# A pairwise-attention kernel: the PSUM layout, the pair layout and the load of the gather table changed together

## The chip, the cores and the metric

The kernel runs on one core of a Trainium2 chip. The metric is device microseconds of one execution, median of several; smaller is better. TensorE (PE) multiplies, VectorE (DVE) and ScalarE (ACT) compute elementwise, GpSimd (POOL) issues indirect gathers, SyncE (SP) issues plain DMAs. Every engine runs its own instruction list in order and meets the others through counting semaphores.

## The reference, cut to what matters

`VOCAB` is 12500, there are 32 fields, a batch of 2048, and embeddings of 64 numbers.

```python
V = emb_v[x]                                  # x: (32, 2048) indices, V: (32, 2048, 64)
iu, ju = np.triu_indices(32, k=1)             # the 496 pairs of fields
VV = V[iu] * V[ju]
hid = relu(einsum('pbk,kh->pbh', VV, at_w) + at_b)      # 64 -> 64
score = einsum('pbh,ho->pbo', hid, at_h)
pooled = sum(VV * score, axis=0)
logit = pooled @ p + w0 + sum(w1[x], axis=0)
prob = sigmoid(logit)
```

Every index outside 0..12499 is wrapped or clamped as the array library does. All arithmetic is float32.

## The kernel before

Because `pooled @ p` is linear, the kernel never forms `VV * score`. It computes the scores of all pairs, and apart from them the Gram products `sum_k p[k] V[i,k] V[j,k]`, multiplies the two and sums over the pairs.

The batch is worked in 32 *fills* of 64 samples (`FILLS`). A fill holds two groups `g` of 16 samples, and each group twice, on the lower and on the upper 64 partitions (`half`). In a fill there are 16 *rounds*: eight steps `s` times two groups, in the order of `ORDER`. Fill 0 and fill 31 are written out, fills 1 to 30 are a loop over two fills.

A round goes through three engines:

- DVE writes the products of one step: `X` (L348, two instructions, one for each of the two pieces that `segments(s)` gives). Step `s` pairs the fields 2s and 2s+1 with all later ones, and the mirror step fills the rest, so a round always has 2 x 512 columns. DVE may be eight rounds ahead (`X_SLOTS`).
- PE multiplies them with `w_sb`: `hidden` (L476), four matmuls of 64 x 64 weights and 512 columns into one of two PSUM slots of `Z` (`Z_SLOTS` 2). Every float32 matmul shows as two passes in the trace, so as two MATMUL rows and two LDWEIGHTS rows.
- ACT adds the bias and applies the relu from `Z` to `H` (L424), 1024 columns. `hidden` of round r waits for the relu of round r-2.

Beside the rounds, PE has in each fill, in program order:

- `scores` (L497): the column `hcol`, placed in a 32-wide weight, times `H`, into the PSUM bank `S`. There are four column tiles of the array (two groups, two halves), each with 128 x 32 weights, and each step needs one matmul a piece and tile: 496 and 16 columns for step 0, 464 and 48 for step 1, and so on to 272 and 240. They stand after rounds 7, 9, 15, and after round 1 of the next fill, two steps at a time.
- `clear_scores` (L485) ahead of the first scores: four bf16 matmuls with zeros open the sums in `S`.
- `grams` (L515): for each of 16 samples and two groups a matmul of 128 x 64 weights (`pV`) and 32 columns (`V`) into the bank `G`, eight of them after each of the rounds 3, 5, 11 and 13.
- `turn` (L455): eight 128 x 128 transposes of the gathered rows of the next fill into the two banks of `TR`, after round 8.

ACT copies `TR` to `V` (L369) after the relu of round 8 and writes `pV` from `TR` (L376) after that of round 15. DVE masks the Gram products (L317), multiplies them with the scores (L323) and sums (L326) in rounds 4, 5 and 6 of the next fill. `S`, `G`, `TR` and the two slots of `Z` are all eight PSUM banks.

POOL gathers the rows of a fill, 16 indirect DMAs of 128 rows (L233), two fills ahead. Fills 0 and 1 gather from `emb_v` itself. The later ones gather from two tables in DRAM, whose rows have the `w1` entry before or behind the embedding (260 bytes): at the start SP loads all of `emb_v` in one DMA of 3104 KB (L191), DVE and ACT join it with `w1` in SBUF (L333, L384), and SP stores both tables (L202), 6.3 MB in all. `w1` of fills 0 and 1 is gathered at the end (L242). The last steps are `linear_term` (L556), the sums of `part` (L566) and a sigmoid (L439).

## Time and profile before

| | |
|---|---|
| median of 3 runs | 920.51 us (919.03 to 921.53) |
| profiled execution | 918.6 us, of which the span of the engines is 916.8 us |
| PE busy | 866.9 us, 95% of the span |
| DVE, ACT, POOL busy | 708.2, 675.2, 563.4 us |
| chain of work that ended last | PE 92%, POOL 4%, DMA 2% |

The profile's page gives busy times, forty slices of the span, the chain that ended last, the costliest groups of instructions and the DMAs. The trace can be asked for any stretch: the chain in order of time, the instructions of one engine merged where they follow each other, the waits, the DMA queues. A busy PE means only that a matmul was in flight: a row's time holds the latency of the pipeline as well, so the pace is read from starts, or from the pieces of the chain.

### The profile page before, as it was taken

How to read it: one execution, taken by the hardware profiler on the slowest of the kernel's cores; microseconds unless marked ns; L12 is line 12 of the kernel's file. 1: busy time of each engine (PE TensorE's matmuls, PEld its weight loads, DVE VectorE, ACT ScalarE, POOL GpSimd, SP SyncE). 2: the span in 40 equal slices, each digit the busy share in tenths (PEclk: the TensorE clock that was granted, in tenths of full speed). 3: DMA queues.
4: the chain of work that ended last, by engine and by line, in shares of the span. 5: the costliest groups of instructions: out<-in, count | busy, mean ns of one | idle time of the engine just before them, and what ended most of it. 6: DMA issues, size and time to landing. Idle time of an engine off the chain costs nothing.

```text
span 916.8 us, 27050 instructions
## 1 busy us (share of the span) xinstructions
PE 866.9 (95%) x10676; PEld 339.1 (37%) x10676; DVE 708.2 (77%) x1179; ACT 675.2 (74%) x771; POOL 563.4 (61%) x584
## 2 busy tenths in 40 slices
PE   0549999999999999999999999999999999999998
PEld 0113333333433333333333333333333333333333
DVE  3555789777778977777898777779877777987772
ACT  3327777787877778787777788777778877777884
POOL 5717767555566765565676556556665555666770
PEclk9878999999999999999999999999999999999999
DMA  8972222222222222222222222222222222222000
GB/s 169 174 143 25 25 26 21 19 19 19 18 21 22 22 19 19 19 19 20 22 23 19 19 19 19 20 21 22 21 19 19 19 19 20 23 19 20 8 1 2
DMA packets 19638, 27.35 MB, mean 30 GB/s; under 512 B 10646, under 2 KB 10662, under 8 KB 18982
## 3 DMA queue, kind: packets, MB, share of 16 engines
q0 software_dynamic: 17408, 17.07, 25.0%
q1 hardware_dynamic: 1566, 10.02, 2.8%
q8 instruction: 11, 0.18, 0.1%
q10 hardware_dynamic: 648, 0.03, 0.0%
q14 instruction: 5, 0.04, 0.0%
HBM read 20.59 MB, written 6.51 MB: 30 GB/s over the span
## 4 chain that ended last, share of the span: by engine, by line
PE 92%; POOL 4%; DMA 2%; issue 1%; DVE 0%; SPq 0%; ACT 0%; POOLq 0%; DVEq 0%
PE Z L476 53%; PE S L497 26%; PE G L515 8%; PE TR L455 4%; POOL rows L233 3%; DMA rows<-in_L_rec_emb_v_dram,idx_stage 2%; PE S L485 1%; PE TR L556 0%; DMA idx_raw<-in_r_x_dram 0%; SPq L188 0%; ACT y_sb L439 0%; DVE prod L323 0%; DVE part L326 0%; POOL idx_stage L221 0%; PE TR L566 0%
## 5 line engine op out<-in xcount | busy, mean ns | idle before, releaser
L424 ACT ACTIVATE H<-Z,bias 128x1024 f32<-128x1024 f32 x512 | 546.5, 1112 | 192.2 <-PE Z L476 191.2
L348 DVE TENSOR_TENSOR X<-V 128x992 f32<-128x992 f32 (+15 forms) x1024 | 640.2, 696 | 24.2 <-ACT V L369 20.8
L233 POOL DMA_INDIRECT rows<-table,idx_stage x480 | 489.2, 1019 | 167.4 <-issue 144.5
L476 PE MATMUL Z<-X,w_sb 64*64 64x512 f32 x4096 | 517.2, 608 | 1.5 <-DVE X L348 1.2
L497 PE MATMUL S<-H,score_w 128*32 128x496 f32 (+15 forms) x4096 | 248.3, 383 | 0.0
L476 PEld LDWEIGHTS Z<-X,w_sb 64*64 64x64 f32 x4096 | 123.7, 131 | 182.4 <-issue 174.8
L497 PEld LDWEIGHTS S<-H,score_w 128*32 128x32 f32 x4096 | 111.2, 110 | 184.4 <-issue 139.8
L323 DVE TENSOR_TENSOR prod<-S,gram 128x512 f32<-128x512 f32 x32 | 22.1, 692 | 159.0 <-PE S L497 159.0
L515 PEld LDWEIGHTS G<-V,pV 128*64 128x64 f32 x2048 | 70.0, 137 | 103.8 <-issue 103.8
L221 POOL COPY idx_stage<-idx 128x16 uint32 (+1 forms) x32 | 7.1, 222 | 143.5 <-ACT w_all L392 122.6
L376 ACT ACTIVATE pV<-TR,pcol 64x512 f32<-64x512 f32 x128 | 87.0, 680 | 2.5
L515 PE MATMUL G<-V,pV 128*64 128x32 f32 x2048 | 84.3, 225 | 0.0
L455 PE MATMUL TR<-ident,rows 128*128 128x128 f32 x256 | 36.9, 289 | 44.6 <-DMA rows<-in_L_rec_emb_v_dram,idx_stage 44.6
L455 PEld LDWEIGHTS TR<-ident,rows 128*128 128x128 f32 x256 | 28.7, 146 | 70.6 <-issue 63.0
L369 ACT COPY V<-TR 128x512 f32<-128x512 f32 x64 | 34.2, 587 | 24.5 <-PE TR L455 24.5
L242 POOL DMA_INDIRECT w_all<-in_L_rec_w_dram,idx x32 | 33.5, 1048 | 9.8 <-issue 9.8
L233 POOL DMA_INDIRECT rows<-in_L_rec_emb_v_dram,idx_stage x32 | 32.7, 1023 | 10.8 <-issue 9.2
L317 DVE TENSOR_TENSOR gram<-G,upper 128x512 f32<-128x512 f32 x32 | 21.8, 681 | 8.1 <-PE G L515 8.1
L326 DVE TENSOR_REDUCE part<-prod 128x512 f32 (+1 forms) x32 | 21.8, 680 | 0.0
L485 PEld LDWEIGHTS S<-zeros 128*32 128x32 bf16 x128 | 3.3, 92 | 26.0 <-issue 26.0
L485 PE MATMUL S<-zeros 128*32 128x512 bf16 x128 | 12.8, 390 | 0.0
L392 ACT COPY w_all<-rows 128x8 f32 x60 | 9.3, 202 | 0.7
(38 smaller groups left out, 42.6 us busy)
## 6 DMA issues: line engine op xcount, KB each, us to landing
rows<-table,idx_stage POOLq DMA_INDIRECT x480
table<-joined SPq DMA_DIRECT2D x2, 1592.5 KB
table<-joined SPq DMA_DIRECT2D x2, 1560.0 KB
raw<-in_L_rec_emb_v_dram SPq DMA_DIRECT2D x1, 3104.0 KB, 11.7
rows<-in_L_rec_emb_v_dram,idx_stage POOLq DMA_INDIRECT x32, 12.3
w_all<-in_L_rec_w_dram,idx POOLq DMA_INDIRECT x32
idx_raw<-in_r_x_dram SPq DMA_DIRECT2D x4, 64.0 KB, 2.2
raw_w<-in_L_rec_w_dram SPq DMA_DIRECT2D x1, 48.5 KB, 13.4
```

What stands on the lines that cost most here:

```text
L233: pool.indirect_dma_start(out=rows[parity][:, g * FILL_M + m, half, c0:c1], out_offset=None, in_=source[half] if joint else source, in_off ...
L242: pool.indirect_dma_start(out=w1_all[:, Q, n:n + 1], out_offset=None, in_=w1, in_offset=at).then_inc(w1_first, 16)
L323: nc.vector.tensor_tensor(prod[:, :, :], S[:, :, :], gram[:, :, :], ALU.mult).then_inc(prod_ready, 1)
L348: last_one = nc.vector.tensor_tensor(xo, vj, vi.unsqueeze(3).to_broadcast(shape), ALU.mult)
L369: nc.scalar.copy(V[parity][:, g, :, :], TR[:, g, :].rearrange("p (b f) -> p b f", f=FIELDS)).then_inc(v_ready, 1)
L376: nc.scalar.activation(pV[parity][k, g, :, half, :, :], TR[k, g, :].rearrange("p (b i c) -> p b c i", c=2, i=FIELDS // 2), ACT.Copy, scale ...
L424: nc.scalar.activation(H[:, r % H_SLOTS, :, :], Z[:, r % Z_SLOTS, :, :], ACT.Relu, bias=bias[:, 0:1]).then_inc(hid_ready, 1)
L455: last = nc.tensor.transpose(TR[:, g, 128 * m:128 * m + 128], embs[:, g * FILL_M + m, 1:1 + 2 * EMB], ident[:, :])
L476: last = nc.tensor.matmul(Z[64 * par:64 * par + 64, r % Z_SLOTS, half, :], w_sb[k, :], X[k, r % X_SLOTS, par, :], start=True, stop=True)
L485: nc.tensor.matmul(S[32 * Q:32 * Q + 32, :, :], zeros[:, 0:32], zeros[:, :].rearrange("p (b j) -> p b j", j=FIELDS), start=True, stop=False)
L497: last = nc.tensor.matmul(S[at:at + 32, :, j0:FIELDS], score_w[:, slot, :], hid.rearrange("p (b j) -> p b j", j=nj), start=False, stop=(s ...
L515: last = nc.tensor.matmul(G[64 * g:64 * g + 64, b, :], pV[parity][:, g, b, :, :, :].rearrange("p h c i -> p (h c i)"), V[parity][:, g, b, ...
```

## The change

- PSUM: `TR`, `S` and `G` go. `Z` gets three slots (`Z_SLOTS` 3, six banks) as a ring over rounds (`z_slot`), in which `turn` takes one place before round 8. Two banks `SG` alternate by fill and hold first the Gram products and then, once DVE has taken those, the scores.
- Waits: `hidden` of round r waits for the relu of round r-3 instead of r-2 (`z_before`), except round 0, 1, 8 and 9 (r-2), and round 10, which waits for the copy to `V`.
- Pairs: `segments` now splits each row of 32 columns in two parts, so that a group's `X` of a step is 16 x 32 in place, and the scores of a step and tile are one matmul of 512 columns. The first one starts the sum (`start=(s == 0)`), so `clear_scores` goes. The order of the rounds is both groups of one step after each other, except in the first half of fill 0 (`FIRST_ORDER`).
- Scores stand after rounds 3 (steps 6 and 7 of the fill before), 7, 11 and 15, with a semaphore step each. All Gram products of the next fill stand in one piece after round 15.
- `grams` has four column tiles in place of two: 64 matmuls of 128 x 32 weights and 32 columns a fill, where there were 32 of 128 x 64 weights. `pV` is one buffer, written by ACT from `V` in two instructions of 1024 columns, before rounds 10 and 14, with a weight column that is zero for the other half (`pmask`). `V` is copied in one instruction.
- DVE: masking takes three instructions (`mask_gram`) instead of one, since the new pair layout wraps around; multiply and sum stand before rounds 10 and 12.
- Table: one table with rows of 66 numbers (`w1`, embedding, `w1`), gathered by an index times 66 plus 0 or 1. SP loads `emb_v` straight into the joined layout, in 12 DMAs of 128 x 8 pieces of 256 bytes, once the rows of fill 0 have arrived, and stores 3.3 MB. POOL writes the two `w1` columns. Fills 0 to 2 gather from `emb_v`.
- POOL: the loop is written out, without the copy of the indices; from fill 4 on each group of four gathers waits for `z_ready` of a round (`PACE`), and one `w1` gather follows each fill.
- `linear_term` uses four row tiles of 32 and stands behind the last scores.

The diff, cut to this:

```diff
-X_SLOTS, Z_SLOTS, H_SLOTS = 8, 2, 8
+X_SLOTS, H_SLOTS, Z_SLOTS = 4, 4, 3
...
 def segments(s):
-    n = FIELDS - 1 - 2 * s
-    return [(s, FIELDS - n, n, 0), (STEPS * 2 - 1 - s, n, FIELDS - n, GROUP * n)]
+    low = 2 * s + 1
+    return [(2 * s, low, FIELDS, 0), (HALF_FIELDS + 2 * s, 0, low, HALF_FIELDS)]
...
+def z_slot(r):
+    return (r if r < TURN_BEFORE else r + 1) % Z_SLOTS
+TURN_SLOT = TURN_BEFORE % Z_SLOTS
+def z_before(r):
+    if r == 2:
+        return -3
+    if r < 2:
+        return r - 2
+    return r - 2 if TURN_BEFORE <= r < TURN_BEFORE + 2 else r - 3
...
+            for g in range(2):
+                sp.wait_ge(first_rows[g], 16 * GATHERS // 2)
+            sp.dma_start(tail[:, :, 1:1 + EMB], last_rows[0]).then_inc(tail_loaded, 16)
+            for k, (c0, c1) in enumerate(HALF_CHUNKS):
+                for c in range(c0, c1):
+                    sp.dma_start(joined[:, c, :, 1:1 + EMB], chunks(emb_v, c, c + 1)[:, 0, :, :]).then_inc(joined_loaded[k], 16)
...
+            gather(2)
+            pool.wait_ge(rows_turned, 1)
+            pool.wait_ge(idx_ready, 4)
+            pool.wait_ge(table_stored, 16 * 3)
+            gather(3)
+            for t in range(4, FILLS):
+                pool.wait_ge(rows_turned, t - 2)
                 pool.wait_ge(w1_kept, 2 * (t - 3))
-                gather(t, parity, table)
+                gather(t, paced=True)
+                gather_w1(1)
...
+                if not first:
+                    dve.wait_ge(v_ready, t)
+                for r, (s, g) in enumerate(FIRST_ORDER if first else ORDER):
...
+                    if r == 8:
+                        mask_gram(t, parity)
+                    if r == 10 and not first:
+                        weigh(t - 1, 1 - parity)
+                    if r == 12 and not first:
+                        sum_pairs(t - 1)
...
+                    xs = X[:, s % X_SLOTS, :, g * COLS:(g + 1) * COLS].rearrange("p c (b j) -> p c b j", j=FIELDS)
...
+                        xo = xs[:, :, :, p0:p1]
...
-            def clear_scores(t, first):
...
             def products(t, parity, first, last):
                 for r in range(ROUNDS):
-                    hidden(t, r, first)
+                    if r == TURN_BEFORE and not first and not last:
+                        pe.wait_ge(hid_ready, ROUNDS * t + TURN_BEFORE - Z_SLOTS + 1)
+                        turn(t + 1, 1 - parity)
+                    hidden(t, r, first, last)
                     if first and r == 3:
-                        turn(0, 0, (1,))
-                        keep_busy(8)
-                    if r == 8 and not last:
-                        pe.wait_ge(pv_ready, 4 * t + 4)
-                        turn(t + 1, 1 - parity)
+                        first_turn(1)
+                    if first and r == 5:
+                        grams(0, 0)
+                    if first and r == ROUNDS - 1:
+                        pe.wait_ge(hid_ready, ROUNDS - 2)
+                        turn(1, 1)
...
+                    if r == ROUNDS - 1 and not last:
+                        grams(t + 1, 1 - parity)
...
+            def grams(t, parity):
+                pe.wait_ge(pv_ready, 2 * t + 2)
+                if not (isinstance(t, int) and t <= 1):
+                    pe.wait_ge(prod_ready, t - 1)
+                for b in range(GROUP):
                     for g in range(2):
                         for half in range(2):
                             at = 32 * (2 * g + half)
+                            last = nc.tensor.matmul(SG[parity][at:at + 32, b, :],
+                                                    pV[:, g * GROUP + b, half, :, :].rearrange("p c i -> p (c i)"),
+                                                    V[parity][:, g * GROUP + b, :], start=(b == 0), stop=(b == GROUP - 1),
+                                                    skip_group_check=True)
+                last.then_inc(gram_ready, 1)
```

PE in the steady loop, from the Gram products behind round 5 (before) through the scores behind round 7. `Z` is `hidden`, `G` the Gram products, `S` the scores:

```order
L515 MATMUL G<-V,pV 64x32 x8
L469 REGISTER_ALU
L476 MATMUL Z<-X,w_sb 64x512 x4
L469 REGISTER_ALU
L476 MATMUL Z<-X,w_sb 64x512 x4
L485 MATMUL S<-zeros 32x512 x4
L497 MATMUL S<-H,score_w 32x16x31 x4
L497 MATMUL S<-H,score_w 32x16 x4
L497 MATMUL S<-H,score_w 32x16x29 x4
L497 MATMUL S<-H,score_w 32x16x3 x4
```

Now, the last two rounds of a fill (14 and 15) with what stands behind them and the first round of the next:

```order
L544 MATMUL Z<-X,w_sb 64x512 x4
L533 REGISTER_ALU
L544 MATMUL Z<-X,w_sb 64x512 x4
L558 MATMUL SG<-H,score_w 32x512 x8
L565 ISA
L572 MATMUL SG<-V,pV 32x32 x64
L533 ISA
L538 REGISTER_ALU
L544 MATMUL Z<-X,w_sb 64x512 x4
```

What moved: the 8 Gram matmuls that stood between pairs of rounds are gone from there, and 64 narrower ones stand once, directly behind scores of the same tile shape; two steps of scores are 8 matmuls where they were 16 and 4 with zeros.

DVE in the steady loop before, rounds 4 to 6, with the masking, the multiply and the sum of the fill before (its waits stand beside the rows):

```order
L317 TENSOR_TENSOR gram<-G,upper 128x512 [waits gram_ready]
L342 REGISTER_ALU
L348 TENSOR_TENSOR X<-V 128x2x464 [waits z_ready]
L348 TENSOR_TENSOR X<-V 128x2x48
L322 REGISTER_ALU [waits gram_masked]
L323 TENSOR_TENSOR prod<-S,gram 128x512 [waits scored]
```

DVE now, from the last product of round 7 to the multiply before round 10:

```order
L410 TENSOR_TENSOR X<-V 128x2x16x7
L364 REGISTER_ALU
L365 TENSOR_TENSOR gram_last<-SG,lower_last 128x256 [waits gram_ready]
L367 TENSOR_TENSOR gram<-SG,upper_first 128x512
L371 TENSOR_TENSOR gram<-gram,gram_last 128x16x16 [waits gram_halves]
L400 REGISTER_ALU
L410 TENSOR_TENSOR X<-V 128x2x16x23 [waits z_ready]
L410 TENSOR_TENSOR X<-V 128x2x16x9
```

What moved: the masking is of the current fill and stands before round 8, in three instructions; the multiply of the fill before stands two rounds later.

## Rows read from the trace of the kernel before

**Rows 1.** The page's busy times, and the granted clock of PE in 40 slices.

```profile
PE 866.9 (95%) x10676; PEld 339.1 (37%) x10676; DVE 708.2 (77%) x1179; ACT 675.2 (74%) x771; POOL 563.4 (61%) x584
...
PEclk9878999999999999999999999999999999999999
```

**Rows 2.** The chain in order of time, one fill: start us, us, engine, tile, line.

```profile
412.88 0.33 PE S L485 x4
413.21 1.76 PE S L497 x32
414.97 1.02 PE Z L476 x8
415.99 1.02 PE TR L455 x8
...
418.03 1.86 PE S L497 x32
419.89 1.88 PE Z L476 x16
421.77 0.59 PE G L515 x16
...
432.44 2.07 PE Z L476 x16
...
439.49 0.33 PE S L485 x4
```

**Rows 3.** Weight loads in time, scores of step 0: start us, us, count.

```profile
413.45 0.12 PEld L497 LDWEIGHTS S<-H,score_w 128*32 128x32 f32 x4 [0.30 <-issue]
413.87 0.18 PEld L497 LDWEIGHTS S<-H,score_w 128*32 128x32 f32 x12 [0.30 <-issue]
```

**Rows 4.** DVE in order of time in one fill.

```profile
410.70 15.06 DVE L348 TENSOR_TENSOR X<-V 128x672 f32<-128x672 f32 x24
425.67 0.68 DVE L317 TENSOR_TENSOR gram<-G,upper 128x512 f32<-128x512 f32 x1
...
432.50 0.69 DVE L323 TENSOR_TENSOR prod<-S,gram 128x512 f32<-128x512 f32 x1 [4.95 <-PE S L497]
...
434.31 0.68 DVE L326 TENSOR_REDUCE part<-prod 128x512 f32 x1
```

**Rows 5.** ACT in order of time in the same fill.

```profile
417.14 1.06 ACT L369 COPY V<-TR 128x512 f32<-128x512 f32 x2
...
428.05 2.79 ACT L376 ACTIVATE pV<-TR,pcol 64x512 f32<-64x512 f32 x4
...
431.20 2.12 ACT L424 ACTIVATE H<-Z,bias 128x1024 f32<-128x1024 f32 x2
```

**Rows 6.** The chain at the start.

```profile
15.54 0.94 POOL rows L233
...
16.79 0.94 POOL rows L233
...
48.47 18.83 DMA rows<-in_L_rec_emb_v_dram,idx_stage
...
82.92 1.88 PE Z L476 x16
```

**Rows 7.** DMA queues from 29 to 66 us: packets, MB, share of 16 engines.

```profile
q0 software_dynamic: 608, 0.62, 51.4%
q1 hardware_dynamic: 562, 6.28, 39.9%
```

**Rows 8.** The same, one steady fill, 412.8 to 439.4 us.

```profile
q0 software_dynamic: 479, 0.50, 23.6%
```

**Rows 9.** All engines in order of time at the end.

```profile
898.70 3.66 PE L556 MATMUL TR<-w_all,pick 128*4 128x128 f32 x32
...
912.08 0.69 DVE L323 TENSOR_TENSOR prod<-S,gram 128x512 f32<-128x512 f32 x1 [4.92 <-PE S L497]
912.81 0.69 DVE L326 TENSOR_REDUCE part<-prod 128x16 f32<-128x512 f32 x1
```

488 lines of the change are left out of this document (247 added, 241 removed).

## The prediction

> **What bounds the kernel now.** I read the page first, then one steady fill. PE is busy 95% of the span and its granted clock is at the upper level (2.4 GHz) from the fifth slice on [rows 1], so after some 90 us the time is PE's own list of work. The chain in order of time shows of what that list is made: one fill lasts from 412.88 to 439.49, 26.61 us, every piece of it on PE [rows 2]. The pieces are worth more than the busy sums, for they hold what it costs to change between kinds of matmul. Two rounds of `hidden` in one block take 1.88, a round alone 1.02 [rows 2]: so a round is 0.86, and a block costs 0.16 more than its rounds. The turn fits (1.02), and so do the scores: 1.86 for two steps whose columns are those of two rounds. So the columns count and not the matmuls: the scores of a step are 16 passes, a round is 8, and both cost the same. Twice in a fill a block of rounds is longer than 1.88 by more than 0.1 (2.07 in the rows, 2.01 the other), a wait for a relu with only two slots.
>
> The other engines have room. DVE writes 12 rounds in 14.97 us (410.70 to 425.67), 1.25 each, and idles 4.95 us [rows 4]. ACT needs 1.06 for a relu in a row, 1.06 for `V`, 2.79 for `pV` [rows 5].
>
> **The change in a steady fill, part by part.**
>
> Zeros: the piece of 0.33 holds an edge; without it the scores behind it cost 1.86 in place of 1.76. Gone: 0.23.
>
> Gram products: four blocks of 0.59, 2.36 in all, go. With them the blocks of `hidden` that they parted join: nine blocks before (after rounds 1, 3, 5, 7, 8, 9, 11, 13, 15), four now, so 5 x 0.16 = 0.80 goes too. The 64 new matmuls stand behind scores of the same tile shape, so I give them no edge. They are 32 passes over four tiles, each with a load of 32 columns and 32 moving columns. The trace has no such pass; what is nearest? Scores of step 0 have 16 moving columns, the same tiles and loads. There, 12 loads (three passes of four tiles) start within 0.18, of which the last load itself is 0.11 to 0.12 [rows 3], so from pass to pass there is 0.03. Below that I see no reason for a gain. Above, the old Gram passes, two tiles with loads of 64 columns, take (0.59 - 0.16)/8 = 0.055. If the load sets the pace (64 columns 0.055, 32 columns 0.03), the new pass is 0.03. I take it: 32 x 0.03 = 0.96, bounds 0.9 and 1.76.
>
> Scores as one matmul: the passes of step 0 with 16 columns cost 0.03 where their columns are worth 0.014, the others nothing. Gone: 0.05. This part of the change, taken alone, brings next to nothing.
>
> Third slot: the longer blocks (0.19, 0.13 and three times 0.05) become 1.88-like. Gone: 0.35. Is nothing later? Write a fill from its start by these pieces: rounds 0 to 3 until 3.59, scores 5.45, rounds 4 to 7 9.04, scores 10.90, turn 11.92, rounds 8 to 11 15.51, scores 17.37, rounds 12 to 15 20.96, scores 22.82, Gram products 23.78. ACT from the turn on: `V` until 13.0, relus 8 and 9 15.1, `pV` (1024 columns, 1.06 like a relu, at most 1.40, half of 2.79) 16.3, relus 10 and 11 18.4, `w1` 18.7, relu 12 19.8, relu 13 20.8, `pV` 22.0. Round 15 begins at 20.1 and needs relu 12: 0.3 to spare. The Gram products begin at 22.8 and need `pV`: 0.8 to spare. Both hold, the first barely: each 0.1 that ACT is later there costs 3 us in 31 fills.
>
> DVE: 16 x 1.25 = 20.0, mask, multiply and sum 0.68 + 0.69 + 0.68 [rows 4], and two new instructions of 256 columns, between 0.34 and 0.68 each: 22.7 to 23.4. Below 23.8, so DVE stays hidden, with 2% to 5% left where it had 19%. Its new waits: the mask waits for Gram products that end with the fill, when eight rounds are still ready; the multiply waits until 5.45 for the scores, and DVE then stands still 1 to 1.5 us with rounds 2 to 9 written ahead. PE needs round 10 at 13.6, DVE has it at about 7.5.
>
> POOL: 17 gathers at 1.25 (16.79 - 15.54 in [rows 6]) are 21.3 of 23.8; rows are due a third of a fill after the last is paced. Hidden.
>
> Sum: 26.61 - 0.23 - 2.36 - 0.80 - 0.05 - 0.35 + 0.96 = **23.78 us a fill**, 2.83 less.
>
> **The start.** Fill 1 begins at 82.92 now [rows 6], held up by the rows of fill 1: the gathers are issued by 48.47 and land 18.83 us later [rows 6], while the two tables (6.28 MB) are stored [rows 7]. Changed: no 3.1 MB load stands before the first gathers, and the table load starts when those have landed. The eighth gather starts at 15.54, so group 0 is there at some 18.5 and not at 24.8, group 1 at 29. The gathers of fill 1 end at 48.5 and those of fill 2 at 69. The table meanwhile: 12,288 pieces of 256 bytes. Bounds for a piece: a gathered row costs 0.236 x 16 x 26.6 / 2048 = 0.049 us of an engine [rows 8], and stored bytes in large packets 0.399 x 592 us / 6.28 MB = 0.010 us per 256 bytes [rows 7]. Over 16 engines that is 8 to 38 us; with gathers beside it, and then 3.3 MB of stores (8 to 16), the table is ready between 50 and 110 us, and I take 65. Then it is later than nothing: POOL has its turn for fill 3 at 69, rows by 91, and PE wants them at 95.
>
> The rows of fill 1 land between 50.5 and 60 in this lighter traffic; turn, `V`, two `pV` and Gram products follow one another there (some 6 us), so fill 1 begins at 56 to 66, I take 60. Fill 2 begins at 84.5, against 109.5 before: 25 us gained, bounds +5 and 30.
>
> **The end.** `linear_term` stood in PE's path with 3.66 us [rows 9]. It now runs with four row tiles while DVE multiplies and sums (0.69 + 0.69). Fill 31 has no turn and no Gram products for a next fill. From the start of fill 31 (82.92 + 30 x 26.61 = 881.2) to the end of the span were 35.6; now four blocks of rounds and of scores 21.8, last scores 1.8, tail 5.1: 28.7. Gained: 7.
>
> **Total**, against the profiled execution (span 916.8, time 918.6): 25 + 29 x 2.83 + 7 = 114, so 804.6. The median is 1.9 above that execution; I say **806**.
>
> **Rivals.**
>
> 1. *A floor per matmul.* The old Gram blocks have 16 passes in 0.43 us if each is counted singly, 0.027 each. If that is a pace of instructions and not of loads, 128 are 3.5 and not 0.96: 26.3 a fill, 806 + 79 = 885. For it: the profile shows no long run of such small matmuls that go faster. Against it: the 12 loads of [rows 3] with their matmuls, but these may be drawn from a filled queue. Chance 0.08. The Trainium skill, page TensorE: Matmul & The Clock Gate, Part 1, "Wait — 56ns, not 53.3ns?", says that starts never come closer than about 25 ns however small the matmul; by it the block would be 3.2 us and the time some 875. The rows with 16 columns speak against applying it to four tiles at once.
> 2. *The pass keeps the pace of the two-tile one*, 0.055: 1.76 for the block, 806 + 31 x 0.8 = 831. Chance 0.10.
> 3. *DVE becomes the bound.* `X` is now written in short runs of 1 to 31 numbers, where a run was whole before. From 1.30 to 1.33 a round on DVE sets the pace; at 1.38 (a tenth more) a fill is 24.7 and the time 834. For it: the new layout. Against it: what it reads was already in such short runs, at 1.25. Chance 0.08.
> 4. *The table is late.* At 100 us instead of 65, gathers end at 122 and turn 3 waits 27 us: 833. Chance 0.06.
> 5. *New waits of ACT and PE* at the tight places above, 0.3 to 0.7 a fill: 815 to 828. Chance 0.05.
> 6. *Slower than before*: the same runs on DVE, but worse. The point from which it decides: 26.6 + 1.0 (start and end gained, a fill's share) - 2.7 (its other work) = 24.9 for 16 rounds, 1.56 a round, a quarter above the rows. At 1.65 the time is about 970. Chance 0.04, of which 0.01 for a time at the point itself.
>
> **How the numbers follow.** The forecast has 0.59, and is itself 796 to 818. The range leaves out the floor per matmul, the slower case and a little of the forecast's own low end, and reaches over cases 2 to 5: 795 to 850. Faster by over 0.3% (what a measurement of this kernel can tell from no change) are all cases but the last: 0.96, within 0.3% 0.01, slower 0.03.
>
> **What will show it.** In the chain of the changed kernel the 16 rounds of a fill should be four pieces of some 3.6 us, two steps of scores with Gram products 2.8; 3.6 and more for Gram products alone is case 1, 1.8 case 2. Steady fills should follow one another by 23.8. If PE idles for `X`, DVE's cadence tells between case 3 and the forecast; if for `H`, it is case 5. PE waiting for rows behind 70 us is case 4. I am wrong in kind if PE shows gaps in the steady fills that none of these names.

## The result, and the profile after

The changed kernel took 868.44 us (864.78 to 874.28, four runs) against 920.78 us (919.03 to 921.53) for the kernel before in the same comparison: 0.944 of the time, 95% interval 0.9385 to 0.9495. It is faster, as forecast, but 62 us above the forecast of 806 and 18 us above the range. The profiled execution took 867.35 us, its span 865.6. The sets of runs in which the experiments were made differ: in some the kernel before took 1383 to 1427 us, not 920, and each experiment is read beside the kernel before of its own set. Where executions of one kernel lay over 1.5% above its fastest, the ratios with an interval leave these out as far as enough others remain; the medians and ranges hold all.

The page after, where [rows 1] stand for before: busy time and share of the span, and PE's granted clock in 40 slices.

```profile
PE 800.9 (93%) x10552; PEld 292.6 (34%) x10552; DVE 722.4 (83%) x1242; ACT 642.8 (74%) x672; POOL 604.9 (70%) x574
...
PEclk9889959999999999999999999999999999999999
```

PE lost 66 us of work and is still the bound. DVE has 14 us more. The sixth slice (108 to 130 us) has the clock down to half.

The chain in order of time, two fills of after, against [rows 2]: start us, us, engine, tile, line. L544 is `hidden`, L558 `scores`, L508 the turn, L572 the Gram products.

```profile
388.65 1.20 PE SG L572 x72
389.85 0.08 issue
389.93 0.38 PE SG L572 x11
390.32 0.42 issue
390.73 3.66 PE Z L544 x32
394.40 1.85 PE SG L558 x16
...
401.70 1.02 PE Z L508 x8
...
413.62 1.12 PE SG L572 x79
414.74 0.06 issue
414.80 3.66 PE Z L544 x32
```

The long blocks, the scores and the turn are what the sum had. The Gram products are not: the block at 388.65 takes 1.66 and is followed by 0.42 in which PE waits for nothing that the profile shows ("issue"); the next block takes 1.12 with 0.06. The starts of single passes show the pauses inside the longer block as gaps of 0.2 to 0.3 us, behind the 50th pass here (the 46th to the 59th in the steady fills) and again some 60 later. I read them as waits of PE for its own instructions: no row names that, but the experiments below bear it out. In 26 steady fills the block took 1.65 us in the middle, and one fill followed another by 24.80 us on the mean where 23.78 was forecast.

DVE in order of time, one piece of the same stretch (against [rows 4]); the bracket is idle time and what ended it.

```profile
420.38 0.69 DVE L378 TENSOR_TENSOR prod<-SG,gram 128x512 f32<-128x512 f32 x1 [1.63 <-PE SG L558]
```

DVE waits here for PE's scores, and not PE for DVE. It sets nothing.

The chain at the start, against [rows 6].

```profile
31.57 5.69 SPq L234
...
58.91 12.07 SPq L234
...
85.71 4.54 DMA joined<-in_L_rec_emb_v_dram
...
90.27 10.10 DMA table<-joined
...
101.16 0.94 POOL rows L268
...
120.94 4.71 DMA rows<-table,joint_idx
...
125.78 1.94 PE Z L508 x8
```

SP needs from 31.57 to 85.7 us to issue the twelve loads of the joined table (5.69 us for the first, 12.07 for the seventh), the last lands at 90.25, the stores at 100.37. Only then does POOL gather the rows of fill 3, which PE awaits for 17.9 us. Its turn takes 1.94 in place of 1.02, at the lower clock level (1.2 GHz, granted clock 0.50), and the four rounds behind it 5.13 in place of 3.66 (0.70 on the mean): PE had stood still just before. Up to here the changed kernel has gained nothing: turn 3 starts at 125.78, in the kernel before at 123.2.

One block has a pause while POOL stands still. The rows of PE for the Gram products behind fill 1:

```profile
95.06 0.64 PE L572 MATMUL SG<-V,pV 128*32 128x32 f32 x48
95.91 0.89 PE L572 MATMUL SG<-V,pV 128*32 128x32 f32 x80 [0.22 <-issue]
```

POOL issued nothing between 66.95 and 101.16, but the stores of the table kept the transfer engines full (1.04 of their time). The longest wait of PE for nothing that the profile shows, 2.99 us from 68.59, also falls into that stretch, with the engines at 0.97 (the last gathers' packets and the loads).

**Where the 62.8 us went** (span 865.6 against the 802.8 that the prediction implies):

| term | forecast | measured | us more |
|---|---|---|---|
| fill 2 begins | 84.5 | 96.9 (its turn's start, less the wait and 10.9) | 12.4 |
| wait of turn 3 for the table's rows | 0 | 17.9 | 17.9 |
| fill 2's start to fill 31's, without that wait | 29 x 23.78 | 29 x 24.88 | 31.9 |
| fill 31 and the tail | 28.7 | 29.2 | 0.5 |

### The profile page after: what moved, and what is told of

The parts are those of the page before. It is cut to its first block, busy times and chain, and to the rows that moved or that the text cites. A ratio compares the mean times of both kernels' runs of the same rounds, so it can differ in the third digit from the quotient of the medians.

```text
span 865.6 us, 26461 instructions
## 1 busy us (share of the span) xinstructions
PE 800.9 (93%) x10552; PEld 292.6 (34%) x10552; DVE 722.4 (83%) x1242; ACT 642.8 (74%) x672; POOL 604.9 (70%) x574
## 4 chain that ended last, share of the span: by engine, by line
PE 84%; SPq 6%; POOL 3%; DMA 3%; issue 2%; ACT 0%; DVE 0%; POOLq 0%
PE Z L544 49%; PE SG L558 25%; SPq L234 6%; PE SG L572 5%; PE Z L508 4%; POOL rows L268 3%; DMA table<-joined 1%; DMA rows<-in_L_rec_emb_v_dram,idx 1%; DMA rows<-table,joint_idx 1%; DMA joined<-in_L_rec_emb_v_dram 1%; DMA idx_raw<-in_r_x_dram 0%; PE Z L627 0%; SPq L220 0%; PE Z L615 0%; SPq L231 0%
## 5 line engine op out<-in xcount | busy, mean ns | idle before, releaser
L268 POOL DMA_INDIRECT rows<-table,joint_idx x464 | 510.4, 1100 | 197.5 <-issue 120.4
L544 PE MATMUL Z<-X,w_sb 64*64 64x512 f32 x4096 | 476.2, 601 | 11.8 <-issue 9.0
L544 PEld LDWEIGHTS Z<-X,w_sb 64*64 64x64 f32 x4096 | 156.8, 133 | 280.2 <-issue 274.7
L558 PE MATMUL SG<-H,score_w 128*32 128x512 f32 x2048 | 247.5, 600 | 0.1
L558 PEld LDWEIGHTS SG<-H,score_w 128*32 128x32 f32 x2048 | 53.8, 109 | 182.0 <-issue 103.8
L436 ACT ACTIVATE pV<-V,pmask 128x1024 f32<-128x1024 f32 x64 | 80.7, 1264 | 0.1
L572 PEld LDWEIGHTS SG<-V,pV 128*32 128x32 f32 x4096 | 50.0, 110 | 31.1 <-issue 26.1
L572 PE MATMUL SG<-V,pV 128*32 128x32 f32 x4096 | 56.6, 200 | 4.0 <-ACT pV L436 1.0
L268 POOL DMA_INDIRECT rows<-in_L_rec_emb_v_dram,idx x48 | 46.3, 964 | 18.0 <-issue 14.2
L508 PE MATMUL Z<-ident,rows 128*128 128x128 f32 x248 | 35.6, 289 | 24.3 <-DMA rows<-table,joint_idx 17.9
L279 POOL DMA_INDIRECT w_all<-in_L_rec_w_dram,idx x48 | 46.4, 966 | 14.6 <-issue 14.6
L508 PEld LDWEIGHTS Z<-ident,rows 128*128 128x128 f32 x248 | 28.0, 146 | 50.3 <-issue 38.6
```

The source lines that it names most:

```text
L268: pool.indirect_dma_start(out=rows[t % 2][:, g * FILL_M + m, half, c0:c1], out_offset=None, in_=source, in_offset=bass.IndirectOffsetOnAxi ...
L279: pool.indirect_dma_start(out=w1_all[:, Q, n:n + 1], out_offset=None, in_=w1, in_offset=at).then_inc(w1_first, 16)
L436: nc.scalar.activation(pV[:, :, half, :, :], V[parity][:, :, :].rearrange("p b (i c) -> p b c i", c=2), ACT.Copy, scale=pmask[:, half:half ...
L508: last = nc.tensor.transpose(Z[:, TURN_SLOT, g, 128 * m:128 * m + 128], embs[:, g * FILL_M + m, 1:1 + 2 * EMB], ident[:, :])
L544: done = nc.tensor.matmul(Z[64 * par:64 * par + 64, z_slot(r), half, :], w_sb[k, :], X[k, s % X_SLOTS, par, COLS * g:COLS * g + COLS], sta ...
L558: last = nc.tensor.matmul(SG[parity][at:at + 32, :, :], score_w[:, s, :], hid.rearrange("p (b j) -> p b j", j=FIELDS), start=(s == 0), sto ...
```

## Experiments

Runs of one set follow each other on one chip and share the kernel before. It took 1383 to 1427 us in the sets of e1 to e16, e19 and e20 (**1400 sets** below) and 916 to 922 us in the comparison above and in the set of e17 and e18 (**920 sets**). The changed kernel stands in the 1400 sets as e5 and e16. The 1400 sets ran on four chips, the set of e17 and e18 on a fifth; whether the chip makes the difference, no run tells. Many expectations give times for the 920 case and met a 1400 set, so there only their direction and the blocks can be held against them.

**e5_after_again and e16_after_third: the changed kernel in 1400 sets.** No edit.

> The changed kernel as it is, once more, so that the kernels beside it stand against it under the same conditions. The kernel before took 1422 us beside the first four experiments and 920 us beside the two kernels' own comparison. If the four columns of a gram block or a round are starved by the supply of TensorE's instructions, this kernel shows it again: gram block of 128 passes 1.65 us where before takes about 920 us, and then 865 to 874 us in all; gram blocks of 4 to 7 us and a steady fill above 30 us where before takes about 1420 us. If the long times beside the first four came from those kernels' own edits, this one gives 868 us beside any time of before.

> The changed kernel as it is, beside the three above. 868 us where before takes 920, 1130 to 1180 us where it takes about 1400.

Measured: 1172.99 us (1168.49 to 1175.51) beside 1423.62, ratio 0.824 [0.821, 0.827]; 1173.61 beside 1418.70, 0.827 [0.826, 0.829]. The steady fill is 34.1 us, the Gram block 6.9. In e5's chain a normal block of that set:

```profile
541.00 0.45 PE SG L572 x39
541.45 0.39 issue
541.84 0.28 PE SG L572 x4
...
545.87 1.17 issue
547.04 0.93 PE SG L572 x39
547.97 6.00 PE Z L544 x32
```

The chain has 39 passes up to the first wait (by the starts of single passes the first gap stands behind the 48th); then PE gets about five at a time, each 0.75 us. The four rounds behind it take 6.00 us instead of 3.6: the granted clock is at its lower level (0.50) from 545.97 to 552.80, behind these pauses. So the pauses of the comparison are here, enlarged: of the 9.3 us that the fill has more, 5.3 are in the block (6.92 for 1.65) and 2.4 behind it. Which blocks have them is told by two other places of the same trace, by the end:

```profile
1099.81 1.86 issue
1101.67 0.21 PE SG L572
...
1115.02 1.33 PE SG L572 x61
...
1140.70 1.12 PE SG L572 x79
```

The block that begins at 1087.03 takes 29.1 us. The next takes 1.12, as the one at 413.6 in the comparison. The engines in a block of the steady part and in these two stretches (busy us and counts of PE, PEld, DVE, ACT, POOL, then clock, DMA share, GB/s):

```profile
574.70:581.70 7.00, 3.01 (x132) 2.27 (x124) 0.93 (x2) 1.29 (x2) 3.89 (x4) 0.89 0.29 19
1087.00:1116.00 29.00, 6.01 (x124) 4.14 (x120) 1.06 (x2) 1.35 (x2) 18.27 (x20) 0.59 0.02 0
...
1140.40:1141.60 1.20, 1.20 (x130) 1.08 (x124) 1.20 (x2) 1.20 (x2) 0.00 (x0) 1.00 0.00 0
```

During the 29 us POOL issues indirect DMAs back to back (the single numbers of `w1`, L279, one each 1.25 us), and the transfer engines are busy for 2% of the time. During the 1.2 us POOL issues nothing. So POOL's indirect DMAs are enough for pauses, with the transfer engines nearly idle. The steady blocks of the comparison say the same: with two indirect DMAs begun in them they take 1.65 us (a few 1.9), whether the engines are busy for 0.09 or 1.09 of the time; the one with one such DMA takes 1.39 (834.72), the one with none 1.11. But they are not the only cause: the pauses at 95.70 and 68.59 there stand beside full transfer engines and an idle POOL.

**e17_no_gathers: no gathers for fills 4 to 31.** It leaves the gathered rows out, and fills 4 to 31 work on those of fills 2 and 3. Two earlier forms of the same edit, e10 and e13, gave no time.

```
                            if t >= 4:
                                pool.dma_start(rows[t % 2][0:1, ...], table[0:1, ...]).then_inc(arrived, 16)
                                continue
                            pool.indirect_dma_start(...)
```

> The changed kernel without the gathers of fills 4 to 31: each is replaced by one transfer of a single row, so that the transfer engines are nearly idle; the other 127 rows of a tile keep what fills 2 and 3 left. If TensorE's instructions come slowly because the gathers' packets (1.1 us each, some 20% of the transfer engines' time) stand ahead of them, the steady fill falls to 24 us or less and the gram block of 128 passes to 1.3 us or less, whatever before takes. If the supply is slow by itself, the fill stays where it was: 33 to 34 us and blocks of 7 us where before takes about 1400 us, 24.8 us and 1.65 us where it takes 920 us.

Measured, in a 920 set: 845.16 us (one run) beside 918.41. Two fills of its chain:

```profile
424.43 1.12 PE SG L576 x79
425.55 0.43 issue
425.98 3.66 PE Z L548 x32
...
448.86 1.12 PE SG L576 x78
449.98 0.06 issue
```

The Gram blocks of fills 3 to 30 take 1.11 to 1.12 us (the last, beside two `w1` gathers, 1.67); fills follow one another by 24.06 and 24.44 in turn, 24.25 on the mean, 0.55 less than in the changed kernel of the comparison, 15 us in all. The rest of the 23 us between the two kernels, 7 us, is not the edit's: turn 3 starts at 118.6 here and at 118.5 in e18 beside it, which has all gathers, but at 125.78 in the comparison. The start varies so much from set to set. The first theory holds, though the fill is 24.25 and not 24 or less: the gathers cause the pauses in the block. In the block at 133.13 POOL issued plain DMAs, one each 0.52 us, and it took 1.12 all the same. It has to be put more narrowly than I wrote it, though. I had their packets' time in mind, and that does not fit: in the changed kernel the block at 437.5 has gather packets of 660 ns on the mean within 3 us around it and the one at 289.2 of 131 ns, and both take 1.65; the one without packets, at 413.6, takes 1.11 (there POOL was in a single gather for 7 us, from 408.40 on). What stays with e17 is a wait of 0.43 behind every second block. The loop's body is two fills, so I put this down to its jump, by its period alone; 0.37 per two fills. The jump by itself cannot be all of it: e18 has the same loop and no such wait (its fills are 25.06 to 25.09), so it seems to cost only behind a long row of narrow passes.

**e18_wide_two_pieces: Gram passes of 64 columns, in two pieces behind the scores of steps 4 and 5.**

```
-    for g in range(2):
-        for half in range(2):
-            matmul(SG[parity][32 * (2 * g + half):..., b, :], pV[:, g * GROUP + b, half, ...], V[...])
+    for g in range(2):
+        matmul(SG[parity][64 * g:64 * g + 64, b, :], pV[:, g * GROUP + b, :, ...], V[...])
+GRAMS_BEHIND = {4: (0, 8), 5: (8, 16)}
```

> The changed kernel with the wide gram passes (64 columns, 64 passes a fill, which alone took 1104 us where before took 1423) in two pieces of 32 passes, behind the scores of steps 4 and 5. If the supply has a store that empties in about 50 passes and refills while the scores run (0.93 us for 8 long passes), the pieces take 1.1 us each with no wait inside, the clock does not fall behind them (the four rounds behind a starved block took 6.4 us in place of 3.66), and a fill is 25 to 27 us: 900 to 970 us. If it is the number of instructions over the whole stretch of scores and grams that counts, nothing changes: 1080 to 1110 us. Splitting the narrow ones in four made a fill 5 to 10 us longer, for which neither has a reason: a third result, 1130 to 1200 us, would say that a gram piece between scores is itself the harm. Where before takes 920 us: 845 to 870 us.

Measured, in the same 920 set as e17: 867.68 us (866.27 to 868.34), ratio 0.9447 [0.9429, 0.9465], what the changed kernel had. Its chain:

```profile
406.63 1.00 PE SG L559 x8
407.62 1.05 PE SG L572 x32
408.68 0.99 PE SG L559 x8
409.67 1.06 PE SG L572 x32
410.73 3.59 PE Z L545 x32
```

Two pieces of 1.05 to 1.06, no pause in the steady fills, 25.07 us a fill, with the gathers in: what the expectation has for the store and for the time (845 to 870 us). So a piece of 32 wide passes is not starved. But 64 wide passes are 2.11 us, a whole microsecond more than 128 narrow ones without pauses, and more than these with them: the fill is 0.27 longer than the changed kernel's, 8 us in all, which the start that is 7 us earlier in this set hides. That is also a price for the tile shapes: 0.033 us a pass of 64 columns, 0.0087 a pass of 32.

**e4_tile64 and e7_tile64: the wide passes in one block.** The edit of e18 without its last line; e4 and e7 are the same kernel.

> The changed kernel with Gram matmuls of the old width, 128 x 64 weights in two column tiles, 32 a fill instead of 64. Theory I: no gaps, but the pass has the old 0.055 us, so the block is 1.76, with two changes of tile shape 0.2 to 0.3 more, together 2.0, against 1.65 and 0.25 to 0.6 of gap now: a fill is 24.7 to 25.0, the time unchanged within 5 us. Rival N (two tiles are simply as good or better, the gaps having another cause): the gaps stay beside the longer passes and the fill is 25.5 or more, 20 us longer in all.

> The changed kernel with the grams' passes at 128 rows by 64 columns (64 matmuls a fill where the change has 128 at 32 columns; the same sums). Half as many TensorE instructions a gram block. Theory (the block is bound by the supply of instructions): the block goes from 1.65 us with its gap behind it to about 1.1 to 1.3 us and the edges shrink, 0.4 to 0.9 us a fill, 850 to 860 us. Rival (the block is bound by the two column tiles that the wide passes then share, 0.59 us for 32 passes in before, so 1.18 for 64, and the gap behind it is a switch between shapes): 0 to 0.5 us a fill, 855 to 868 us. The prediction's own price for the narrow passes (0.96 us a block) says that this one is slower by 0.2 us a fill: 875 us.

Measured in 1400 sets: 1090.58 us beside 1422.57 (ratio 0.767 [0.762, 0.771]) and 1103.92 beside 1423.62 (0.770 [0.766, 0.774]), the best there is in 1400 sets: e4 is 82 us below e5, and the two fastest runs of e7 (1092.45 and 1098.76) are 77 below it, on the same chip. Steady fill 31.0 us for 34.1, block 3.3 for 6.9; the rounds behind it still take 6.42 us in e7. The granted clock falls behind the shorter pauses too, but is low for 3.4 us only (516.0 to 519.4), which is worth 1.7 of the 2.8 us more; the rest is not explained. With half as many instructions the block takes half the time.

**e3_split4 and e6_split4: narrow passes in four pieces of 32** (behind the scores of steps 4 to 7); the same kernel twice.

```
+GRAMS_BEHIND = {4: (0, 4), 5: (4, 8), 6: (8, 12), 7: (12, 16)}
```

> The changed kernel with the Gram matmuls of a fill in four pieces of 16, one behind each step of scores after rounds 15 and 3; nothing added or left out, the tile shape around them is the same. Theory I (64 small matmuls in a row run dry of instructions: in the trace of the changed kernel a block has 54, then 60 passes at 9 ns each, with gaps of 0.2 us between and a longer gap behind every second block): the gaps go, 32 passes of 35 ns are 1.1 us, a steady fill falls from 24.8 to 23.9, the time by 25 to 30 us to some 840. Rival W (the gaps are waits for pV or for DVE): they stay, 24.8 a fill; or DVE, whose mask now waits until after round 3, becomes late and a fill gets longer.

> The changed kernel with the gram columns of a fill issued as four pieces of 32 passes each, one behind each of the scores of steps 4, 5, 6 and 7, instead of one block of 128 passes at the end of round 15 of each fill. Theory (TensorE runs out of its own instructions after some 54 passes at 0.009 us apiece, so a long block of short passes pays gaps of 0.2 us and one more to the next round): pieces of 32 passes take 0.28 to 0.35 us with no gap inside, 0.3 to 0.8 us less a fill, 10 to 25 us in all, so 845 to 858 us where this kernel's parent takes 868. Rival (the gaps belong to the passes, wherever they stand, or each piece pays 0.16 us to change from the rounds' passes to the grams' and back): no gain or up to 0.6 us a fill lost, 868 to 888 us.

Measured: e3 1410 us (1396 and 1424) beside 1423, unclear; e6 1382.93 (1368.96 to 1391.98) beside 1423.62, ratio 0.964 [0.959, 0.968]: some 200 us slower than e5. Both theories miss. From e6's chain:

```profile
706.67 0.99 PE SG L559 x4
707.66 0.10 PE SG L574 x2
707.76 0.10 issue
...
708.40 0.10 PE SG L574 x4
708.50 1.12 issue
709.62 0.27 PE SG L574 x3
```

These are the third piece's end and the fourth piece, behind the scores of step 7. PE waits already while these scores run, and then over all of the fourth piece (707.66 to 722.65); the first three took 0.28 to 0.37 each. That the 0.99 us of scores between the pieces are too short to fill a store again would fit, but is not shown. That the pieces make it worse than one block is measured and not explained.

**e14_two_score_matmuls: the merging of the scores undone.**

```
-    last = matmul(SG[parity][at:at + 32, :, :], score_w[:, s, :], hid)
+    for p0, p1 in ((2 * s + 1, FIELDS), (0, 2 * s + 1)):
+        last = matmul(SG[parity][at:at + 32, :, p0:p1], score_w[:, s, :], hid[:, :, p0:p1])
```

> The changed kernel with each score matmul of 512 columns issued as two of fewer columns, as before the change: 128 score passes a fill instead of 64, the same columns. Where before takes about 1400 us (steady fills of 40.5 us for 784 loads and passes of TensorE before, 34.0 us for 656 of after: 19.3 of them in a us both times), the instruction count decides by this theory: 784 again, 40.6 us a fill, 31 x 6.6 = 205 us slower than the changed kernel, 1340 to 1390 us. Rival (the pace is that of the short gram passes only, and the wide scores cost nothing): 1140 to 1185 us. Where before takes 920 us: 0 to 0.3 us a fill, 868 to 878 us.

Measured: 1343.93 us (1336.83 to 1350.35) beside 1418.70, 170 us more than e16 in the same set; the steady fill is 39.7 us for 34.1. The number fell into the expected range, but the reason given was partly wrong: I had miscounted. The kernel before has no 784 loads and passes a fill but 664, the changed one 656 (the pages count 10676 and 10552 passes), so their difference cannot come from the count. What holds is that 64 matmuls more, with the same columns in all, cost 5.6 us a fill where the supply is slow. The fill of before has 6.5 more than the changed one's in such sets (e9), so much of the gain there hangs on this part, which I had priced at 0.05. It is not a share of the 6.5, though: with e15's 2.3 the parts add up to more than the whole.

**e15_z_two_back: the third slot not used to run ahead.**

```
def z_before(r):
-    if r == 2:
-        return -3
-    if r < 2:
-        return r - 2
-    return r - 2 if TURN_BEFORE <= r < TURN_BEFORE + 2 else r - 3
+    return r - 2
```

> The changed kernel with each round's wait put back to the relu of two rounds ago, as before the change: three slots are there, but the third is not used to run ahead. Where before takes 920 us, the relu (1.12 us each, two a round with 0.1 us between) then ends 0.1 to 0.2 us too late for the round in stretches without scores: 0.5 to 2.8 us a fill, 884 to 955 us. Where before takes about 1400 us the supply of instructions hides it, if that is the bound: within 10 us of the changed kernel there.

Measured: 1257.42 us (1255.59 to 1257.95) beside 1418.70, ratio 0.886 [0.884, 0.888]: 84 us more than e16, 36.4 us a fill. I expected it to be hidden and it is not: the slot is worth 2.3 us a fill there. Its chain has waits for issue in front of single rounds, which e16 has in fewer places (171 waits in front of rounds, 133.6 us in all, for 62 and 34.9):

```profile
528.28 0.66 issue
528.94 1.09 PE Z L540 x8
```

With slots to spare a pause for instructions is worked off; without them it is added to the wait for the relu. This reading fits the rows, but no run tells it from others. What the slot is worth in a 920 set was not measured.

**e9_before_again: the kernel before, profiled in a 1400 set.** No edit.

> The kernel before as it is, with a profile of its own under the conditions of the first eight experiments (there it took 1423 us, not 920). Theory (TensorE's instructions come at a fixed slow pace there, some five gram passes in 0.75 us, so the time goes where many short instructions stand in a row): its blocks of 16 gram passes take more than their 0.59 us, up to 2.3 us each, eight a fill, and the chain shows waits for issue ahead of the gram line; the 32 loads of zeros of a fill, which take no time in the array, cost too; about 16 us more a fill, nearly all as issue waits of TensorE. Rival (all engines are slow there, or the clock is low throughout): the rounds' 1.02 us for eight passes and the vector engine's 693 ns grow in the same proportion, 1.55 times.

Measured: 1382.63 us beside 1388.87 for the same kernel. The fill is 40.65 us for 26.61. My place for it was wrong: the Gram blocks still take their 0.59, as they did before. The pauses are around the turn and the scores:

```profile
602.65 0.37 PE TR L455 x2
603.02 0.43 issue
603.45 0.55 PE TR L455 x3
```

and behind them the clock is at its lower level (granted 0.50): the scores from 612.23 on take 3.57 us for 32 passes, where 1.86 is usual. The matmuls between, 2.68 us for four passes at 606.30, are slower than the clock explains. DVE's `X` takes 693 ns as ever, so it is not the whole core that is slow.

**e1_plain4, e2_plain2 and e8_plain2: one fill more, or one less, gathered from the embeddings themselves.** `PLAIN_FILLS = 4`, and `PLAIN_FILLS = 2`, with the gathers moved to their side of the wait for the table; e2 and e8 are the same kernel.

> The changed kernel with the rows of fill 3 gathered from emb_v too (and w1 of fill 3 with the late ones), so that nothing waits for the table before the rows of fill 4. Theory T (the table, stored at 100 us, holds up the turn of fill 3 at 125.8, where PE had nothing to do for 17.9 us): that wait goes, the turn of fill 3 comes at about 108, the time falls by 16 to 20 us to some 849; the turn of fill 4 may wait a little, since the gathers of fill 3 now run beside the load and the table is later than 100. Rival G (the late time sits in the steady fills, and the start only shifts): less than 5 us.

> The changed kernel with the rows of fill 2 from the table, so POOL issues no gather between the rows of fill 1 and the stored table. Theory E (indirect gathers from emb_v hold the DMA engines, packets of 2048 bytes at 1.1 us, and the load of 256-byte pieces gets what is left): with the gathers ended at about 48 us the load runs at the rate seen after 80 us, 3161 pieces in 5 us, the table is stored by 75 to 80, and the time moves by -10 to +2 us. Rival S (SyncE needs 4.5 us to issue each of the 12 loads, whatever else runs): the table is stored at 100 as before, the turn of fill 2 comes at some 122 instead of 83, and the time is 15 to 20 us longer.

> The changed kernel with only fills 0 and 1 gathered from the embedding table itself, and fill 2 already from the joined table; the Pool engine then issues a third less of the slow gathers while the table is copied. Theory (the gathers of the third fill, 1.1 us a packet, hold the transfer engines while the table's small pieces wait, which is why the last load landed at 90 us and the gathers of fill 3 began at 101): the table is complete by 75 to 85 us, fill 2 starts at 95 to 105 us instead of 83, fill 3 straight behind it at 120 to 125 instead of 125.8; the total is 862 to 869 us. Rival (the table's copy is bound by its own issues, whatever the gathers do): the table is ready at 100 as before, fill 2 turns at 122 us and fill 3 at 147: 888 to 892 us.

Measured: e1 1197.99 us (ratio 0.842 [0.838, 0.847]), e2 1154.38 (0.812 [0.807, 0.816]), e8 1157.17 (0.813 [0.811, 0.815]), all beside 1423; e5 on the same chip 1173. Fill 3 turns at 152.0, 156.7 and 156.9 against 152.2, so fill 3 is not earlier in any; in 1400 sets PE comes later than the table, which is no bound there. The table itself was earlier with fewer gathers, as theory E has it: in e2 and e8 the loads and stores were through by 72 to 73 us, in e5, on the same chip with the 16 gathers of fill 2 beside them, at 89. In e8 POOL goes on with

```profile
73.66 0.94 POOL L268 DMA_INDIRECT rows<-table,joint_idx  x1 [26.98 <-DMA table<-joined]
```

The 25 us that e1 loses and the 16 to 19 that e2 and e8 gain lie in the end: from the last turn but one to the last e1 needs 78 us, e5 55, e2 and e8 32. There POOL issues 64, 48 or 32 DMAs for `w1` in a row (`gather_w1`), and the Gram block waits all through, as seen in e5. What a different `PLAIN_FILLS` does to fill 3 in a 920 set remains open.

**e12_early_loads: the table's loads do not wait for the first rows.**

```
-            for g in range(2):
-                sp.wait_ge(first_rows[g], 16 * GATHERS // 2)
```

> The changed kernel with one edit: the 13 loads of the table are issued at the program's start and do not wait for the rows of fill 0. Theory (the loads' small pieces wait behind the gathers' packets, so the table is late, and the rows of fill 3 with it): with 25 us more the table is stored by 75 to 85 us in place of 100, and where before takes 920 us fill 3 turns at 107 to 112 us in place of 125.8, so 852 to 856 us in all. Rival (what the loads gain the gathers lose, since both go through the same transfer engines): fill 0 turns 5 to 12 us later and fill 3 at 120 or later, 865 to 875 us. Where before takes 1423 us the changed kernel took 1173 and had no wait for the table at fill 3: between 1160 and 1180 us.

Measured, in a 1400 set: 1140.52 us (1132.13 to 1144.81) beside 1388.87, ratio 0.823 [0.820, 0.827], the ratio of e5. Fill 0 turns at 22.7 for 18.8, fill 3 at 152.4 for 152.2: neither theory's gain. The loads are issued from 5.04 to 42.7, 20 us sooner than in e5. But POOL still waits for the table until 91.7:

```profile
91.70 0.94 POOL L266 DMA_INDIRECT rows<-table,joint_idx  x1 [22.36 <-DMA table<-joined]
```

From 45 to 70 us, with gathers under way, the queue of the stores moved 2.07 MB (23.3% of the engines' time; the gathers had 71.3%). In the changed kernel it moved 2.88 MB in the 10.1 us from 90.3, with no gathers. So loads and stores both went slowly while gathers ran, and starting the loads sooner moved the wait from the one to the other.

**e11_wide_grams_fill2_table, e20_early_wide_grams and e19_early_four_pieces: combinations.** e11 is the edits of e7, e8 and e12 at once, e20 those of e7 and e12, e19 those of e6 and e12.

> Three edits to the changed kernel at once, as a version that may beat both: gram passes 64 columns wide (half the TensorE instructions of a block), fill 2 gathered from the joined table already, and the loads of the table issued without waiting for the first rows. Where before takes 1423 us: the wide grams gave 69 us of 1173, the table for fill 2 gave 16 us, and if both add, 1085 us; the earlier loads give 5 us more if the table then is ready by 95 us, 1080 us. If the rows of fill 0 are late because the loads stand ahead of them, 1090 to 1100 us. Where before takes 920 us: 845 to 860 us.

> Two edits to the changed kernel: the table's loads issued at the start, and the gram passes 64 columns wide, 64 a fill, in one block. Start as in the run beside it. Steady, where before takes 920 us: a block of 1.84 us without waits (the shortest that was seen) gives 24.06 + 0.73 = 24.8 us a fill, so no gain over the changed kernel's 24.8 from this edit, 845 to 860 us in all; with the pauses still there 25.2 us, 860 to 870 us. Where before takes about 1400 us: 1060 to 1100 us.

> Two edits to the changed kernel: the table's loads issued at the start, and the narrow gram passes in four pieces of 32 (behind the scores of steps 4, 5, 6, 7). Where before takes 920 us: if the table was late because its loads waited 25 us for the first rows, fill 3 turns by 105 to 110 us instead of 118 to 126, 8 to 20 us less; if the gathers of fills 0 to 2 lose the same time, fill 0 turns 4 us or more later and fill 3 at 115 or later. Steady: pieces of 32 take 0.28 to 0.30 us with no wait inside and no wait for instructions at the loop's edge, a fill is 24.1 to 24.3 us against 24.8; if pieces of this kind make the supply worse (as where before took 1423 us: 34 to 44 us a fill), 25 us or more. Together 835 to 850 us if both hold. Where before takes about 1400 us: 1340 to 1390 us.

Measured, all in 1400 sets: e11 1121.06 us (1092.28 to 1128.94) beside 1388.87, too scattered for a ratio (the fastest run alone would be 0.786); e20 1105.90 (1103.36 to 1121.85) beside 1415.45, 0.782 [0.779, 0.784]; e19 1380.99 (1354.89 to 1402.74), 0.976 [0.971, 0.981], which its scatter leaves unclear. None adds to the wide passes alone (0.770). I have found no version that is better than the changed kernel in a 920 set; the narrow pieces and the earlier loads were only seen in 1400 sets.

## Why the prediction missed

**The bound and the kind of gain: right.** PE was the bound and is still. Rounds in four long blocks (3.66 and three of 3.59; 3.59 forecast), scores at 1.85 for two steps, the turn at 1.02: these terms (-0.23 zeros, -0.80 edges, -0.35 slot) hold to 0.07 us a fill. They are read from the sum of the fill, not from a run of each alone.

**The Gram products: price of the pass nearly right, the block wrong.** 0.03 us for four tiles was forecast; without gathers (e17) 128 passes take 1.11 us, 0.035. The missing piece is that such a stretch outruns the supply of instructions while POOL makes indirect DMAs: 1.65 in the comparison. The step that failed is the term 0.96, which prices the block by the pass's own pace alone and has no wait in it or behind it. Its size looks like rival 2's (1.76 a block), but e17 shows that it is not that case: the pass had the fast pace. Rival 1, a floor per matmul (3.5 us a block), is excluded: 1.11 us is 0.0087 us a pass, 128 of them. The Trainium skill, page TensorE: Matmul & The Clock Gate, Part 1, "Wait — 56ns, not 53.3ns?", has starts never closer than about 25 ns; for passes that go to four tiles in turn these rows show a third of that, and the measurement decides.

The 1.02 us that a steady fill (24.80) has over 23.78 are: 0.55 pauses with the gathers (e17), 0.15 the pass (1.11 for 0.96), 0.06 at the edge to the rounds and 0.19 more at the loop's jump (0.43 less 0.06, every second fill), 0.07 the first block's 3.66. In the kernel before the fills follow one another by 26.61 all alike, so nothing there told of the loop's edge. Over 28 fills that is 29 us; 3 more come from the fill behind the long wait, at half clock.

**The start: the failed step with the largest price.** The prediction had the table at 65, "between 50 and 110", and took the low part. It was 100.4. The working gave the load 8 to 38 us; it took 58.7 (31.57 to 90.25), and the stores 10.1 of their 8 to 16. The estimate used what one piece costs an engine (0.010 to 0.049 us); the pieces themselves took 0.018 to 0.019, well inside. What failed is that it put next to nothing on the gathers beside the load. While gathers ran, the 256-byte pieces crept: 395 to 1883 in each 5 us between 40 and 80, and 3152 in the 5 us from 85 on, when the gathers had stopped; a gather's packet of 2048 bytes took 1.1 to 1.2 us of an engine. With the 16 gathers of fill 2 gone from beside it (e2 and e8, in 1400 sets) the table was there 16 to 17 us sooner than in e5, which shows the cause there; e12 shows the same from the other side. Rival 4 (table at 100, wait of 27 us) had this case at 0.06, and it came with 17.9 us, since PE was itself late. With bounds of 50 and 110 it should have had far more.

Fill 2 began 12.4 us later than forecast for a second reason. The rows of fill 1 landed at 59.2, in the forecast's 50.5 to 60 but at its end, where I had taken 54: 5.2. From turn 1 to the first round of fill 1 (66.69) PE needed 7.5, for "some 6": 1.5. And from there to turn 2 (83.25) 16.6, for 10.9: 5.7, of which this row of PE in order of time tells the half.

```profile
71.58 4.26 PE L544 MATMUL Z<-X,w_sb 64*64 64x512 f32 x22 [2.99 <-issue]
```

PE stood 2.99 us with nothing to wait for that the profile shows, and its 22 passes then took 4.26 where 2.5 are usual, at a granted clock of 0.64 on the mean. The forecast had no such wait either.

**The end:** 7 us gained as forecast (29.2 us from fill 31 on for 28.7; `linear_term`'s four row tiles are 0.98 us).

**DVE and ACT: right.** 693 ns for `X` as before, so the short runs cost nothing; `pV` takes 1.26 (1.06 to 1.40 forecast), and PE did not wait for a relu in the steady part. Rivals 3, 5 and 6 did not happen.

**The range** took each rival alone. Rivals 2 and 4 together, 831 and 27, would have been 858, and something of both kinds happened. They concern different stretches of the program and nothing made one exclude the other.

**What stays open:** why a kernel's supply of TensorE's instructions is that much slower in some sets of runs; how POOL's indirect DMAs reach it, and whether full transfer engines without them (95.70 and 68.59 in the changed kernel) do the same (in e2 and e8 a block with POOL idle and the engines full, at 59.8 and 59.3, had no pause, but was at the lower clock); why four narrow pieces are worse than one block; and what merging and third slot are each worth in a 920 set. A remedy that the traces suggest, keeping POOL's gathers out of the stretch from the last scores to the first rounds, was not tried.

## What to carry to other kernels

Before a change packs short instructions together, ask not only how long each takes but how many stand in a row and what else is issuing meanwhile: here the first 44 to 59 passes were nearly always free of it, and beyond them the pace was the supply's, which POOL's indirect DMAs slowed. Price a stream of small pieces beside gathers by how it moved while gathers ran, not by the time of a piece. And when two unlikely rivals concern different stretches, add them before the range is drawn.

## What the runs showed of the hardware

- TensorE passes on four column tiles of 32 with 32 moving columns follow one another in 0.0087 us (1.11 us for 128); on two tiles of 64 it is 0.033 us (1.05 us for 32).
- With POOL issuing indirect DMAs, PE pauses after 44 to 59 such passes in nearly all steady blocks; then gaps of 0.2 to 0.3 us in the 920 sets, about five passes each 0.75 us in the 1400 sets, 29 us for a block at e5's end, while the transfer engines were 2% busy. With no indirect DMA begun in it the block took 1.11 to 1.12 in both kinds of set (the changed kernel and e17); the one exception is that of fill 2 in the comparison (1.54, with a pause of 0.22, the transfer engines full of the table's stores).
- Every second block of 128 short passes, by its period where the loop over two fills jumps, cost PE 0.37 us more before the next round; behind two pieces of 32 wide passes (e18) it cost nothing.
- 12,500 pieces of 256 bytes took 58.7 us to load beside 29 indirect gathers, and 3152 of them went in 5 us without: the load and the 3.3 MB of stores were through at 72 to 73 us without the gathers of one fill and at 89 with them (e8 and e5).
- Behind a block with seven pauses of 0.4 to 1.2 us (e5) the granted clock was at its lower level for 6.8 us, behind one with three of 0.35 to 0.38 (e7) for 3.4 us; the four rounds there took 6.0 and 6.4 us and not 3.6. Behind blocks with pauses of 0.1 us and one of 0.4 (the comparison) it stayed at the upper level.
- One kernel can take 920 or 1420 us, and one change be worth 0.944 or 0.825 of the time, by the set of runs alone, and the sets were on different chips; the order of before and after was the same in both, but that of two variants was not (wide passes in one block are some 77 us ahead of the changed kernel in e7; in two pieces, in a 920 set, they are 0.27 us a fill behind it in e18).
